# A 12-pass selective scan on one core: GpSimd's u and norm jobs ahead of the step's product

## The reference

```python
xz = u @ W_in; xr, z = split(xz)               # 96 -> 192 + 192 channels
x = silu(causal_conv4(xr) + conv_b)
dt, Bm, Cm = split(x @ W_x)                    # 6, 16 and 16
delta = softplus(dt @ W_dt + b_dt)
h = exp(delta * A_n) * h + (delta * x) * B_n   # along the sequence, for each of 16 states n
y = sum_n h * C_n + x * D
out = (y * silu(z)) @ W_out
```

## Time and profile before

| | us |
|---|---|
| median of 3 runs (lowest, highest) | 2034.77 (2033.21, 2038.48) |
| profiled execution, its own time | 2036.81 |
| span of its profile, first to last instruction | 2034.9 |
| GpSimd busy | 1937.6 (95% of the span) |
| TensorE busy | 1833.8 (90%) |
| VectorE busy | 1787.9 (88%) |
| ScalarE busy | 1149.4 (56%) |

### The profile page before, as it was taken

How to read it: one execution, slowest core, us unless ns; L and a number is a source line. 1 busy time by engine, 2 the same in 40 slices (tenths; PEclk the granted TensorE clock), 3 DMA queues, 4 the chain that set the end, 5 groups by cost and what they waited for, 6 DMA issues and landing times. The chain is left out here.

```text
span 2034.9 us, 16945 instructions
## 1 busy us (share of the span) xinstructions
PE 1833.8 (90%) x4972; PEld 686.9 (34%) x4972; DVE 1787.9 (88%) x1063; ACT 1149.4 (56%) x1179; POOL 1937.6 (95%) x853
## 2 busy tenths in 40 slices
PE   7899889898899899899899889989989988987778
PEld 3333333333343233233333333323323323332332
DVE  3889897868989988987898997998798999699998
ACT  4657565657657446654756745744584574554332
POOL 1999999999999999999999999999999999999997
PEclk9899999999999899999999999999999999999899
DMA  5558558665766877676776787776666677667676
GB/s 148 206 203 210 208 206 208 207 225 180 191 240 217 202 231 255 174 233 212 210 199 219 214 222 233 228 201 243 212 172 207 224 208 215 233 219 207 210 224 153
DMA packets 127623, 427.86 MB, mean 210 GB/s; under 512 B 18524, under 2 KB 23020, under 8 KB 127532
## 3 DMA queue, kind: packets, MB, share of 16 engines
q1 hardware_dynamic: 127532, 426.79, 68.9%
HBM read 416.29 MB, written 6.29 MB: 208 GB/s over the span
## 5 line engine op out<-in xcount | busy, mean ns | idle before, releaser
L987 POOL TENSOR_TENSOR ring<-ring,c_ring 128x1024 f32<-128x1024 f32 x575 | 1346.2, 2369 | 38.3 <-DVE ring L932 33.0
L560 PE MATMUL y_ps<-ring,wp 128*128 128x512 f32 x2304 | 1148.3, 616 | 10.9 <-DVE yv_rows L912 4.5
L932 DVE TENSOR_TENSOR_SCAN ring<-a_ring,b_ps 128x1024 f32<-128x1024 f32 x368 | 841.1, 2286 | 31.6 <-issue 0.5
L560 PEld LDWEIGHTS y_ps<-ring,wp 128*128 128x128 f32 x2304 | 428.1, 194 | 522.5 <-issue 439.8
L932 DVE TENSOR_TENSOR_SCAN ring<-b_ps,b_ring 128x1024 f32<-128x1024 f32 x208 | 471.1, 2274 | 75.1 <-ACT b_ps L732 26.5
L980 POOL TENSOR_TENSOR b_ring<-u_ab,b_ring 128x1024 f32<-128x1024 f32 x161 | 381.9, 2372 | 8.9 <-DMA b_ring<-bc_rows 8.9
L541 PE MATMUL b_ps<-b_in,sel 96*64 96x512 bf16 (+1 forms) x1020 | 230.3, 402 | 143.5 <-DVE ring L932 141.8
L732 ACT ACTIVATE a_ring<-delta_ab,wp 128x1024 f32<-128x1024 f32 x223 | 251.9, 1140 | 158.4 <-DVE ring L932 155.2
L897 DVE TENSOR_TENSOR b_ps<-u_ab,b_ps 128x1024 f32<-128x1024 f32 x223 | 270.3, 1212 | 64.6 <-PE b_ps L541 56.5
L732 ACT ACTIVATE b_ps<-delta_ab,wp 128x1024 f32<-128x1024 f32 x161 | 179.8, 1117 | 208.3 <-DVE ring L932 207.8
L725 ACT ACT_TABLE_LOAD x186 | 238.6, 1283 | 52.7 <-DVE ring L932 49.8
(11 more groups left out here) (97 smaller groups left out, 849.5 us busy)
## 6 DMA issues: line engine op xcount, KB each, us to landing
c_ring<-bc_rows SPq DMA_DIRECT2D x384, 512.0 KB, 4.7
c_ring<-bc_rows SPq DMA_DIRECT2D x384, 256.0 KB, 4.4
b_ring<-bc_rows SPq DMA_DIRECT2D x161, 512.0 KB, 5.3
b_ring<-bc_rows SPq DMA_DIRECT2D x94, 256.0 KB, 5.4
out<-io SPq DMA_DIRECT2D x16, 192.0 KB, 5.0
bc_rows<-bc_out SPq DMA_DIRECT2D x22, 128.0 KB, 5.3
io<-x SPq DMA_DIRECT2D x6, 384.0 KB, 6.2
b_in<-parts SPq DMA_DIRECT2D x24, 96.0 KB, 2.3
```

The costliest lines, as they stand in the source:

```text
L560: nc.tensor.matmul(half(y_ps[:, :], j), ident, half(ring[:, g % RING, :], j), start=(n == 0 and kind == FWD), stop=(n == NS - 1)).then_inc ...
L932: nc.vector.tensor_tensor_scan(out=h, data0=a, data1=b, initial=0.0, op0=ALU.mult, op1=ALU.add).then_inc(h_ready, 1)
L987: nc.gpsimd.tensor_tensor(r, r, c, ALU.mult).then_inc(g_ready, 1)
```

## The change

In each step GpSimd does the jobs that the tables give to the step ahead of the step's product, in place of behind it. It is one line, the order of the phases in GpSimd's queue:

```diff
 PE_ORDER = ("ahead", "sum_0", "jobs", "sum_1")
 ACT_ORDER = ("ahead_a2", "ahead_a", "jobs")
 SP_ORDER = ("ahead_b", "ahead_c", "jobs")
-POOL_ORDER = ("ahead_b", "product", "jobs")
+POOL_ORDER = ("ahead_b", "jobs", "product")
 DVE_ORDER = ("take_0", "scan", "take_1", "ahead", "jobs", "last")
```

## The result

The changed kernel took 2040.52 us (median of 13 runs, 2037.72 to 2050.18); the kernel before, timed again beside it, 2035.75 us. The ratio is 1.0032, 95% interval 1.0019 to 1.0045: 6.5 us slower (0.0032 x 2035), with 3.9 to 9.2 us in the interval. The two medians lie 4.8 us apart, the means 6.5, since the runs of the changed kernel spread over 12.5 us and those of before over 5.3. The forecast was 2037.9 us, "no change that can be told", range 2031.5 to 2049. The time lies in the range, but that range is 17.5 us wide. The loss is about twice the 3.1 us of the sum, just over the 0.3% that was taken as the bound of what can be told, and its interval leaves out zero.

A forecast was written before the change was run, and what follows sets the result against it. TensorE was taken to set the pace at the head of a pass, VectorE behind it, GpSimd beside them; 1.5 + 0.8 + 0.8 = 3.1 us on the profiled 2036.81, less 2.04 to the median, gave 2037.9 us, range 2031.5 to 2049.

The forecast's parts named there:

- the 3.1 us of the sum: Net loss forecast: 1.5 us at the end of pass 8, 0.8 at the end of pass 5, 0.8 in pass 1.
- The new waits: Moved jobs ask for their input 2.31 us sooner, so GpSimd stands still, among others at s26 in passes 3 to 9.
- The other jobs find their input there: Jobs beyond the listed u at s26, u at s35 in pass 5 and norm at s11 in pass 1 add no wait.
- sum of 13.0 us: All the time GpSimd is held up by moved jobs, in passes 1 and 3 to 9; the bound if all counts.
- What becomes of them: GpSimd's lateness from s26 on is swallowed in the next pass, where TensorE sets the pace, except in three places.
- The pass ends: Late products make TensorE wait at the ends of passes 5 and 8: 0.8 and 1.5 us.
- u at s35, 0.8 us: Pass 5: u already waits for delta; products behind it 1.5 to 2.3 us late, costing 0.8 us at the pass end.
- The gain of norm: TensorE's waits for norm at s28 of passes 5 and 8 (0.78 and 0.26 us) go, but nothing is counted.
- Pass 1: Norm at s11 waits 2.1 us net; the product of s25 has 1.2 us of room, so 0.8 us is lost.
- The named signs: GpSimd's new waits for ScalarE, no TensorE wait for norm, smaller GpSimd wait for VectorE, TensorE 1.5 us more near pass 8's end.
- the slow rival: GpSimd binds throughout: its lateness reaches VectorE at the pass heads, all 13.0 us count, 2047.8 us; chance 0.27.
- The rival of earlier inputs: TensorE's 1.04 us and ScalarE's 7.4 us of waits for norm are on the path: 2026.3 us; chance 0.07.

The follow-up runs named there:

- e2: Kernel before with only the u jobs moved ahead of their step's product, all norm jobs left behind it: ratio 1.0070, +14.2 us.
- e5: Kernel before with only the u of tile 0 (s26, in pass 2 s28; nine jobs) ahead of its product: ratio 1.0047, +9.6 us.
- e6: Kernel before, order unchanged, GpSimd held 1.69 us by three dummy memsets ahead of the product of s26 in passes 3 to 9: ratio 1.0038, +7.7 us.
- e10: Kernel before, order unchanged, GpSimd held by three dummy memsets at s26 of passes 3, 4, 6, 7 and 9 alone: ratio 1.0006, +1.2 us.
- e9: Kernel before, order unchanged, GpSimd held by three dummy memsets at s26 of passes 5 and 8 alone: ratio 1.0028, +5.7 us.
- e3: Changed kernel with the u of tile 0 put back behind its product, the other 39 jobs ahead: ratio 1.0021, +4.3 us against the kernel before.
- e12: Kernel before with only the u of tile 1 (s35) ahead of its product, from pass 2 on: ratio 1.0021, +4.3 us.
- e4: Kernel before with only the norm jobs of s27 and s28 in passes 2, 5 and 8 ahead of their product: ratio 1.0008, +1.6 us.
- e1: Kernel before with only the 16 norm jobs ahead of their step's product, all u left behind it: ratio 1.0016, +3.3 us.
- e7: Changed kernel with the dt jobs of tile 0 one step earlier on TensorE and ScalarE: ratio 1.0078, +15.9 us against the kernel before.
- e8: Kernel before, old GpSimd order, with the dt jobs of tile 0 one step earlier on TensorE and ScalarE: ratio 1.0064, +13.0 us.
- e11: Kernel before with only the norm jobs of s39 and s40 in passes 2, 5 and 8 ahead of their product: ratio 1.0006, +1.2 us.

## Why the prediction was right, and where its sizes were off

**The new waits: right.** Waits at s26 in passes 3 to 9 were foreseen, 2.43 and 2.02 us gross in passes 8 and 9; measured 2.51 and 2.35. For norm at s11 3.73 us were foreseen, 3.8 came. "The other jobs find their input there" missed three: u at s35 in passes 2 and 10 (1.45 and 1.25 us) and norm at s22 in pass 1 (0.6 us); and the wait of before at s35 in pass 5 went. In the sum of 13.0 us, the 1.5 us for pass 5 are the lateness at s35; the 0.9 us at s26 of that pass are not in it.

**Swallowed by the next pass: not as it was argued.** The step "What becomes of them" said that GpSimd's lateness from s26 on reaches nobody until the pass ends, and that TensorE sets the pace at the head of the next. It does reach VectorE there: at the scan of s3 in pass 7 the difference to before grows by 0.9 to 1.4 us in all five runs with GpSimd held at s26 of pass 6 (the changed kernel, e2, e5, e6, e10), and by -0.5 to +0.1 us in the eight others. For five holds of 1.69 us most of it is given back (e10, 1.2 us). For the longer waits of the changed kernel this is not shown: between s12 of pass 6 and s24 of pass 8 its trace loses 2.6 to 3.4 us more than runs with the old order, a stretch that the prediction put at nothing. In passes 5 and 8 a hold in the old order costs 5.7 us (e9), since norm stands a few places behind it and TensorE close behind norm. The prediction looked at norm in the changed order alone, where norm is early, and there it was right: no wait for norm is left. Norm's own move pays for u there. u of tile 0 costs 9.6 us alone (e5), but the changed kernel is only 2.2 us above the one without it (e3), and these intervals overlap.

**The pass ends: the places were right, the sizes too small.** The prediction had 0.8 + 1.5 = 2.3 us for the ends of passes 5 and 8. In the trace they lose 3.14 and 3.11 us, where runs with the old order there lose at most 0.31: about 6 us. At the end of pass 8 TensorE waits for products by 2.25 us more and starts its convolutions 3.5 us later, for 1.5 us forecast. The mis-sized term is u at s35, 0.8 us: it measured 4.3 us (e12, 2.4 to 6.1), since b for s42 is queued behind it too. The prediction had b in the queue there, but held that VectorE does not need GpSimd until the head of the next pass. The gain of norm was put at nothing. e4, with that gain alone, is not faster (+1.6 us, -0.4 to +3.5), and in its trace 1.15 and 0.86 us go again at the two ends; but most of the 2.61 us in pass 5 was a slow stretch in the trace of before, so there was less to swallow than the table suggests. Pass 1 was foreseen at 0.8 us; the table shows 0.84, and the four runs with norm ahead in pass 1 (the changed kernel, e1, e3, e7) have 0.84 to 3.55 us there, the nine others -1.46 to +0.67.

**What was luck.** That the time came out near the forecast rests on parts that were off in both directions: the ends of the passes cost more than the sum said, the heads of passes 7 and 8 were not in it, and norm ahead took away what u ahead costs without it (14.2 us against 6.5 for both).

**The named signs.** No wait of TensorE for norm was left, as said. The wait for VectorE should have shrunk by most of what the new waits add; it shrank by 9.9 us of 21.8. By the prediction's own test this is half-way to the slow rival. GpSimd bound throughout would have cost all 13.0 us; the measured 6.5 is half of it, and 13.0 lies outside its interval. The Trainium skill, Perfetto Trace Analysis, section Identifying the Most-Contended Engine, says to optimize the engine with the highest occupancy first. Taken as a price for every hold of that engine, this does not hold here: in e10 the products of the engine that is busy for 95% come 5.6 us later for 1.2 us of time, in e9 2.3 us later for 5.7.

**The rival of earlier inputs** fell: TensorE's 1.04 us of waiting for norm are gone and ScalarE's 7.4 us are down to 4.3, and the time is longer.

**Open.** How the 6.5 us split between the three groups of jobs is not settled: norm (3.3), u of s35 (4.3) and the first u (9.6) do not add up, and e1, e3 and the changed kernel lie too close for their intervals. Norm alone costs 3.3 us; its parts at s27 and s28 (1.6) and at s39 and s40 (1.2) can't each be told from nothing, and pass 1's part was not run alone. Where e8's 13.0 us come from is shown in one place of one pass only.

## What to carry to other kernels

Before moving work ahead on an in-order engine, look at when its input is ready, and then follow everything behind it in the queue for as far as the lateness lasts, each with the slack of its own consumer: here instructions further back in the queue (norm, b of s42) mattered at least as much as the one that changed places. An engine that is busy for 95% can be held for little in one stretch and for more than the hold in another; a few small dummy operations put in one place at a time measure that directly, if the idle time that they fall into is taken off. A difference between two traces is worth little before the same stretch has been looked at in runs that change nothing there. And where two moves meet in one queue, run each alone: one may be paying for the other.

## What the hardware showed that I had not expected

A short wait of TensorE can cost more than its length through the clock, but the same wait does not always bring the clock down. In six places of the traces of e2, e5, e6 and e9, TensorE waits 1.65 or 1.66 us for norm at s28 of pass 5 or 8. In two of them (pass 5 of e2, pass 8 of e5) the granted clock of the next 14 us is 1.00, and from VectorE's scan of s24 to that of s36 it is 43.98 us. In the four others it is 0.76, so part of the stretch runs at the lower level of 1.2 GHz, and it is 46.7 to 47.3 us. With a wait of 0.22 us and the clock at 1.00 (pass 5 of e10) it is 42.38. So the wait costs 1.6 us, and the clock another 2.7 to 3.3 where it falls. Shorter waits go either way too: 0.78 us in the kernel before with 0.88, 0.70 us in e11 with 1.00. What decides it is not shown; no run sets the clock by itself.
